# Thirty-six scatters of sorted rows moved from the update stage to the end of the rank stage of a four-layer graph network

## What is computed

```python
edge_index = jnp.stack([src, dst])
h = jnp.maximum(_layernorm(x, axis=-1), 0.0)
x = x + _L0_gnn_ref(h, edge_index, edge_attr_64, ...)   # edge MLP, sum at dst, node MLP
h = jnp.maximum(_layernorm(x, axis=-1), 0.0)
x = x + _L1_gnn_ref(h, edge_index, edge_type_64, ...)   # attention with 4 heads over the edges into a node
h = jnp.maximum(_layernorm(x, axis=-1), 0.0)
x = x + _L2_gnn_ref(h, edge_attr_64, ..., edge_index)   # attention over the edges out of a node
h = jnp.maximum(_layernorm(x, axis=-1), 0.0)
x = x + _L3_gnn_ref(h, edge_index, ...)                 # graph attention and a gate
```

## Time and profile before

| | us |
|---|---|
| three runs before | 3916.58, 3914.08, 3915.79; median 3915.79 |
| the profiled execution, its own time | 3911.31 |
| span of the profiled execution, first to last instruction | 3909.5 |
| PE, DVE, POOL busy in the span | 2789.2, 2932.6, 2590.5 |
| rank stage, first instruction to first of the next stage | 142.3 to 433.2 |
| make stage | 433.2 to 549.5 |
| update stage | 1284.8 to 1638.5 |

### The profile page before, as it was taken

The page is one execution under the profiler, slowest core; times in us unless marked ns, Lnnn a source line. Parts: engine busy times, 40 slices in busy tenths (PEclk is TensorE's granted clock), DMA queues, the critical chain, the costliest instruction groups (busy, mean ns, idle before and its releaser), DMA issues. The chain is left out here.

```text
span 3909.5 us, 59454 instructions
## 1 busy us (share of the span) xinstructions
PE 2789.2 (71%) x13639; PEld 1620.7 (41%) x13639; DVE 2932.6 (75%) x6788; ACT 940.4 (24%) x2734; POOL 2590.5 (66%) x2675
## 2 busy tenths in 40 slices
PE   5446789999998899699999977799999640000007
PEld 4345432333332688456666544466665320000004
DVE  7897548888887333299999966699999666666664
ACT  0011112222221233245545522222222120000004
POOL 0487567777766577677777756677777337777772
PEclk8555699999999899799999988899999865555559
DMA  4487447777776333377777732688787424444440
GB/s 199 131 262 241 113 125 211 212 213 210 207 205 166 81 68 70 90 211 212 211 211 212 204 79 72 193 238 237 238 239 226 103 70 108 108 108 108 108 103 34
DMA packets 430094, 629.44 MB, mean 161 GB/s; under 512 B 254381, under 2 KB 290834, under 8 KB 428832
## 3 DMA queue, kind: packets, MB, share of 16 engines
q0 software_dynamic: 168064, 505.00, 45.4%
q1 hardware_dynamic: 252608, 94.37, 9.7%
q10 hardware_dynamic: 9312, 28.71, 2.3%
HBM read 549.09 MB, written 78.40 MB: 161 GB/s over the span
## 5 line engine op out<-in xcount | busy, mean ns | idle before, releaser
L1291 POOL DMA_INDIRECT edge_ring<-tab,edge_rec x480 | 468.5, 976 | 179.1 <-issue 133.4
L2350 POOL DMA_INDIRECT state<-tab,edge_rec x480 | 453.9, 946 | 157.1 <-issue 145.9
L1976 PE MATMUL edge_psS<-edge_terms,ident 128*128 128x256 f32 x1952 | 472.1, 385 | 19.0 <-DVE edge_psS L2020 18.8
L2522 PE MATMUL gate_psT<-ident,gate_hb 128*128 128x128 f32 x50 | 9.9, 286 | 612.0 <-ACT gate_hb L2483 612.0
L1976 PEld LDWEIGHTS edge_psS<-edge_terms,ident 128*128 128x128 f32 x1952 | 361.0, 192 | 202.6 <-DVE edge_psS L2020 152.3
L1857 POOL DMA_INDIRECT state<-tab,edge_rec x360 | 340.5, 946 | 122.7 <-issue 105.1
L1857 POOL DMA_INDIRECT state<-tab,edge_feat x360 | 340.5, 946 | 121.4 <-issue 106.4
L1358 PE MATMUL edge_psX<-state,ident 128*128 x720 | 375.2, 630 | 38.7 <-DVE edge_ring L1393 38.6
L1995 PE MATMUL edge_psX<-state,ident 128*128 128x512 f32 x720 | 350.7, 611 | 18.4 <-DMA state<-tab,edge_feat 16.8
L1393 DVE TENSOR_TENSOR edge_ring<-edge_psX,edge_ring 128x1024 f32<-128x1024 f32 x240 | 294.0, 1225 | 74.8 <-PE edge_psX L1370 27.1
L2052 DVE TENSOR_TENSOR edge_prod<-edge_psX,state 128x1024 f32<-128x1024 f32 x240 | 293.9, 1225 | 17.3 <-PE edge_psX L1995 13.9
(11 more groups left out here) (499 smaller groups left out, 6104.1 us busy)
## 6 DMA issues: line engine op xcount, KB each, us to landing
sorted_d<-state SPq DMA_DIRECT2D x8, 2312.0 KB
feat_d<-state SPq DMA_DIRECT2D x32, 528.0 KB, 5.7
edge_feat<-sorted_d SPq DMA_DIRECT2D x116, 136.0 KB
edge_feat<-feat_d SPq DMA_DIRECT2D x113, 132.0 KB
state<-tab,edge_rec POOLq DMA_INDIRECT x840
state<-src_rows ACTq DMA_DIRECT2D x26, 512.0 KB
state<-low_rows ACTq DMA_DIRECT2D x26, 512.0 KB
edge_ring<-tab,edge_rec POOLq DMA_INDIRECT x600
```

Source lines behind the costliest of these rows:

```text
L1291: pool.indirect_dma_start(out=ring[:, k, s, :], out_offset=None, in_=S["tab0"][:, :], in_offset=bass.IndirectOffsetOnAxis(ap=rec[:, k, R_S ...
L1976: last = pe.matmul(so_far, S["ident"][:, :], terms[:, s, :], start=False, stop=(s == QE - 1), skip_group_check=True)
L2350: pool.indirect_dma_start(out=ring[:, k, s, :], out_offset=None, in_=S["tab3"][:, :], in_offset=bass.IndirectOffsetOnAxis(ap=rec[:, k, R_S ...
```

## The change

Nine groups (36 scatters) are taken from the 57 of update and given to rank; make, edge0, update and project keep their places in the list, 9 groups further on. In rank the ten operations that turn places into row numbers become a function, called once behind the twelfth look-up for the first 48 columns and once at the old place for the other 368. A ring of three slots for the rows is cleared at the stage's start, and the tile `begins` goes to a piece of a shared tile to make room. SP loads the nine groups between the store of layer 0's records and that of layer 2's; POOL scatters them behind the gathers of `x` and waits for their landing.

```diff
-MAKE_GROUPS, ROW_TURNS, UPDATE_GROUPS = 12, 11, 57
+RANK_GROUPS, MAKE_GROUPS, ROW_TURNS, UPDATE_GROUPS = 9, 12, 11, 48
+RANK_COLS = -(-RANK_GROUPS * HERE // COLS) * COLS
...
-        begins = ph.sb("begins", [P, NB, NB])
+        begins = S["H"].rearrange("p b f -> p (b f)")[:, 5 * TILE:5 * TILE + NB * NB].rearrange("p (a b) -> p a b", b=NB)
...
+        scattered = RowScatter(ph, S, A, 0, RANK_GROUPS, 3)
+        s_placed = ph.sem("first_places_ready")
...
                     sp.dma_start(S["rec_d0"][:, bass.ds(t * P, P), :], rec[:, :, :]).then_inc(s_st, 16)
+                sp.wait_ge(s_placed, 1)
+                scattered.load(sp)
                 hold(sp, s_n1, 1)
...
                                             in_offset=bass.IndirectOffsetOnAxis(ap=S["x_row"][:, b:b + 1], axis=0)).then_inc(s_x, 16)
+                scattered.some(pool, 0, RANK_GROUPS * HERE)
                 pool.wait_ge(s_x, 16 * NB)
+                scattered.finish(pool)
...
                 begin0(step)
+                scattered.clear(dve)
                 step(dve.tensor_copy(src_h[:, :, :], folded(S["src_i"][:, :])))
...
+                def find_places(own):
+                    to, near, far = S["place_i"][:, own], place[:, own].bitcast(I32), S["src_i"][:, own]
+                    step(dve.tensor_tensor(to, place[:, own], above[:, own], ALU.add))
...
                 for t in range(MAKE_AT):
                     look_up(t)
+                find_places(slice(0, RANK_COLS))
+                dve.nop().then_inc(s_placed, 1)
...
                 for t in range(MAKE_AT, TURNS):
                     look_up(t)
-                to, near, far = S["place_i"][:, :], place[:, :].bitcast(I32), S["src_i"][:, :]
...
+                find_places(slice(RANK_COLS, EDGE_C))
...
-        scattered = RowScatter(ph, S, A, MAKE_GROUPS + ROW_TURNS, UPDATE_GROUPS, 2)
+        scattered = RowScatter(ph, S, A, RANK_GROUPS + MAKE_GROUPS + ROW_TURNS, UPDATE_GROUPS, 2)
```

More of the change, by code:

```diff
@@ L52 @@
 ROW_RING = 5
-MAKE_GROUPS, ROW_TURNS, UPDATE_GROUPS = 12, 11, 57
-PROJECT_GROUPS = EDGE_C // HERE - MAKE_GROUPS - UPDATE_GROUPS - ROW_TURNS
+RANK_GROUPS, MAKE_GROUPS, ROW_TURNS, UPDATE_GROUPS = 9, 12, 11, 48
+PROJECT_GROUPS = EDGE_C // HERE - RANK_GROUPS - MAKE_GROUPS - UPDATE_GROUPS - ROW_TURNS
+RANK_COLS = -(-RANK_GROUPS * HERE // COLS) * COLS
 TURNS_MIN = -(-(-(-N_EDGES // (QE * P))) // AQ)
@@ L827, in look_up @@
                     step(dve.tensor_reduce(place[:, cols(t)], look, AX.X, ALU.add))
+                def find_places(own):
+                    to, near, far = S["place_i"][:, own], place[:, own].bitcast(I32), S["src_i"][:, own]
+                    step(dve.tensor_tensor(to, place[:, own], above[:, own], ALU.add))
+                    step(dve.tensor_scalar(near, to, P - 1, 2, ALU.bitwise_and, ALU.logical_shift_left))
+                    step(dve.tensor_scalar(far, to, 7, QE - 1, ALU.logical_shift_right, ALU.bitwise_and))
+                    step(dve.tensor_tensor(near, near, far, ALU.bitwise_or))
+                    step(dve.tensor_scalar(far, to, 9, 9, ALU.logical_shift_right, ALU.logical_shift_left))
+                    step(dve.tensor_tensor(near, near, far, ALU.bitwise_or))
+                    step(dve.tensor_scalar(far, to, 7, None, ALU.logical_shift_right))
+                    step(dve.tensor_scalar(near, near, no_far[:, 0:1], None, ALU.mult))
+                    step(dve.tensor_scalar(far, far, many[:, 0:1], None, ALU.mult))
+                    step(dve.tensor_tensor(to, near, far, ALU.add))
                 low(0)
@@ L1069, in make_tables @@
         n_loads = 3
-        ROWS_AT, ROWS_N = 0, 0 if gat else MAKE_GROUPS
+        ROWS_AT, ROWS_N = RANK_GROUPS, 0 if gat else MAKE_GROUPS
         ROWS_FIRST = 8
@@ L1225, in edge_mlp @@
         feat = ph.sb("feat", [P, RING_0, QE, EROW])
-        scattered = RowScatter(ph, S, A, MAKE_GROUPS, ROW_TURNS, 1)
+        scattered = RowScatter(ph, S, A, RANK_GROUPS + MAKE_GROUPS, ROW_TURNS, 1)
         dense = ph.sb("dense", [P, 2, QE, ED])
@@ L2109, in project_out @@
         ROWS_N = PROJECT_GROUPS * HERE
-        scattered = RowScatter(ph, S, A, MAKE_GROUPS + UPDATE_GROUPS + ROW_TURNS, PROJECT_GROUPS)
+        scattered = RowScatter(ph, S, A, RANK_GROUPS + MAKE_GROUPS + UPDATE_GROUPS + ROW_TURNS, PROJECT_GROUPS)
         N = NextTables(ph, S, A, 2, Y, rows[:, 1, :], rows[:, 2, :])
```

## The result

The changed kernel takes 3929.86 us (median of seven runs), the kernel before 3915.83 in the same comparison: 14.0 us more, a ratio of 1.0031 with a 95% interval of 1.0021 to 1.0042, that is 8 to 16 us slower. (One of the seven runs, at 4396 us, showed a mean TensorE clock of 0.684 instead of 0.84 and is left out of the ratio; the median of the other six is 3929.2, 13.4 us more.) The profiled execution of the changed kernel took 3931.44 us by its own time. That is the longest of the six, and the profiled execution before, 3911.31, is shorter than all seven runs before: the two profiles lie 20.1 us apart, not 13 or 14.

What follows compares the result with a forecast made beforehand. DVE's look-ups end rank; PE's rounds pace update, POOL's backlog ends it by about 11 us. Rank +25.1 and update -11.0 make +14.1 on 3915.79: 3930 us, range 3920 to 3936.

Steps and rivals of the forecast that it cites:

- Who ends rank: End of rank: POOL's last scatter starts at 450.0, 19.6 us after the store that ended the stage until now.
- third rival: Rank: scatters go only while DVE is idle, so the last starts 18.4 us later, 3948 us; chance 0.05.
- the gather of the earlier trace: Rank: a gather took 11.21 us while DVE ran 25 additions, cited for DVE holding POOL off.
- The tail behind POOL's last DMA: End of rank: make starts 8.2 us after the last scatter's start, bounds 5.7 and 10.4; rank +25.1 us.
- four stages: Next stage's start after POOL's last indirect DMA: make 10.09, update 10.35, project 6.66, make of layer 3 5.70 us.
- first rival: End of rank: no POOL tail, make starts 2.74 us after the last scatter; net +8.6 or +4.9; chance 0.16.
- The sentences on the Trainium skill's rule: End of rank: a branch to a target outside held pages forces a fetch, paid openly behind POOL's last scatter; unproven.
- The gain in update: End of update: POOL's backlog goes, the last store starts at 1617.1 instead of 1628.13, -11.0 us; rounds stay 12.53.
- the extremes: Sum of rank and update: +6.5 to +17.3 us, with -14.7 in update if its tail shrank to project's 6.66.
- second rival: Update: POOL sets the pace, 36 scatters fewer save 45.8 us, net -20.7, 3895 us; chance 0.10.
- What I costed at nothing: Rank: DVE's 2.3 us from the split and SP's later loads and record store, both ended before POOL at 450.
- The sum: Whole kernel: +25.1 in rank and -11.0 in update make +14.1 us, median 3929.9.

Runs made afterwards that it cites:

- the rank part alone: Changed kernel with all 57 groups kept in update, nine of them also scattered in rank; 3944.32 us, ratio 1.0059 against the kernel before.
- the second experiment: Kernel before with update scattering 48 groups instead of 57, the nine groups left out and scattered nowhere; 3900.43 us, ratio 0.9951.

## Why the prediction was right, step by step

The forecast was 3930, +14.1 us; measured +14.0 (+13.4 by the six runs of the ratio), within 8 to 16. The mechanism held, and two terms were off in opposite directions.

**Who ends rank: right.** POOL's list runs on behind DVE's: eleven scatters start behind DVE's end at 436.4, and 15 behind 430.4, where the stage's work ended before. With four groups the same list is over in time, with six its last scatter starts 2.7 us behind SP's store, with nine 10 us. The scatters' times were right to 1.2 us: first at 403.0 (expected 404.2), last at 449.2 (450.0). Beside look-ups they were 1.35 apart (expected 1.34), so the third rival, in which scatters go only while DVE is idle, is out here. The rule that I quoted from the Trainium skill, page "SBUF — State Buffer", section "SBUF: two separate sides", costs these scatters at most 0.07 us each, while the gather of the earlier trace rows paid ten. My quotation left out the condition that this section of the Trainium skill sets, that DVE's operation runs in a two-port mode or has two SBUF inputs; which of the look-ups' operations meet it was not tested.

**The tail behind POOL's last DMA: size too small, cause open in the prediction and now told in part.** I took the mean of four stages, 8.2 us, and 10.4 as the upper bound; it was 10.56, beyond the bound. So rank lost 26.5 and not 25.1. The first rival (2.7 us) is out. The sentences on the Trainium skill's rule (page "Runtime: NRT & Kernel Launch", section "Instruction fetch mechanics") pointed at the wrong instruction: POOL's branch takes 38 ns, all of the way from the barrier into make 1.1 us, and no DMA queue moves a packet there, while 7.02 us are a drain ahead of the barrier. In rank that drain grows by 0.082 us with each scatter of the row. I could have read this before: the row of L561 stood in the trace of the kernel before, with 4.06 us hidden under DVE. So did the drains of the four stages whose tails I averaged: 6.02 of 10.09 us, 6.10 of 10.35, 2.42 of 6.66 and 2.09 of 5.70. What is left beside the drain is 3.6 to 4.3 us in each, and 3.5 in rank.

**The gain in update: right in kind, its tail left out.** The last store came 11.6 us earlier in the stage (expected 11.0), and PE's rounds stayed (12.58 against 12.53). But I kept the old tail, and put its shrinking, -3.7, only into the extremes. It did shrink, to 6.66, the very figure of project that I had named. Its drain fell from 6.10 to 2.52 us, and did so too with the nine groups left out (2.51), while with the rank part alone it stayed at 6.11; so it goes with the list of update, not with rank. Update gave 15.3, not 11.0. The second rival, POOL's pace, is out by the second experiment.

**What I costed at nothing.** SP's 27 loads never held POOL: no scatter waited more than 0.31 us. DVE's delay was 5.9 us where I wrote 2.3, under POOL's cover here. With four groups, where that cover is gone, rank is 6.6 us longer; 2.4 of it is the split, and the rest lies partly in the spread of the stage. That estimate was too low and did no harm by the luck of which engine ended last.

**The sum.** The two misses, +1.4 in rank and -4.3 in update, make +11.2 from the two stages. Some 2 to 3 us of the measured 13.4 to 14.0 then lie in the spread of stages that did not change, which the runs don't resolve (the interval is 8 us wide). So the agreement of 14.1 with 14.0 is closer than the working deserved, and in part luck.

## What to carry to other kernels

An engine's idle time in a stage is room only up to the end of the work that covers it: count the issues that fit, take off the engine's own way out of the stage, and move no more than that. An engine that is full but not the bound returns only the backlog with which it reaches the stage's end. Here two groups removed from update gave 10.8 us and nine 15.3, while rank paid 6.6 us for four groups and 26.5 for nine.

## What the runs showed of the hardware

POOL's way out of a stage behind indirect DMAs is not only the landing of the last: its queue showed a drain of 4.07, 5.38, 6.03 and 7.02 us with 25, 41, 49 and 61 of them in rank's closing row, repeated to within 6 ns between kernels, and neither 2 nor 15 us without work ahead of the last made it shorter. While it ran in the changed kernel's rank, no DMA queue moved a packet. What it counts in other stages stays open: in update it was 6.10 us with 57 groups, 5.94 with 55, 5.04 with 54, 4.97 with 53, 4.07 with 51 and 2.52 with 48, which is no straight line, and in project 2.42 with 24, 2.75 with 26, 3.16 with 27 and 3.56 with 28.
